# Second aggregation, router, dense mixture and node features in one stage over pairs of node tiles; half the edge products in the edge stage

## The chip, the cores and the metric

One core of one Trainium2 chip. The metric is the device time of one launch in microseconds (us); lower is better. In the profile PE is TensorE, PEld its weight loads, DVE is VectorE, ACT is ScalarE, POOL is GpSimd, and SP issues most transfers.

## The reference, cut to what matters

6250 nodes (49 tiles of 128, `NT`) with 256 features; 106250 edges sorted by destination. Four layers, each added to `x`:

```python
h = relu(segment_sum((LN(x) @ W1)[src] * w, dst) + b1)          # conv 1, hidden 128
x = x + segment_sum((h @ W2)[src] * w, dst) + b2                # conv 2
f = LN(x)                                                        # mixture of 6 experts, top 2
top_w, top_i = top_k(softmax(relu(f @ rw1 + rb1) @ rw2 + rb2), 2)
x = x + sum_k softmax(top_w)[k] * (relu(relu(f @ e1 + c1) @ e2 + c2) @ e3 + c3)[top_i[k]]
n = mish(LN(x) @ Wd.T + bd)                                      # node features
msg = relu(n[src] + mish(edge_attr @ We.T + be))                 # 106250 edges x 256
x = x + mish((n + segment_sum(msg, dst)) @ Wo.T + bo)
x = x + moe8(LN(x))                                              # 8 experts, top 2, H = 512
```

`mish(z)` is `z * tanh(softplus(z))`.

## The kernel before

Everything is in float32, so that one multiplication of the source is two records in the trace. Edges are padded to 840 columns of 128 and handled in groups of four columns (`CG`), 208 groups (`GROUPS`) in all. The gathering stages loop over steps of six groups (`SLOTS`), 34 full steps and one of four (`TAIL`). POOL gathers the source rows of a group with four indirect transfers into one of six buffers, and goes on when DVE has released a buffer (`slot_free`). A group's destinations lie in one window of 64 nodes (`W`): DVE builds one-hot matrices (`one_hots`), TensorE multiplies them with the gathered rows (`segment`), and DVE adds the result to a table in SBUF at the group's place (`add`). The places are loaded from SBUF into registers six at a time (`places_of`). The whole loop runs `passes` times, once unless a group's span is wider than 64.

`build` calls the stages one after another, with a barrier between them:

- `stage_begin`: loads `x` (all 49 tiles stay in SBUF), normalises it, multiplies with `W1` and stores the support table; DVE finds each group's first destination.
- `stage_conv(0)`: first aggregation. Beside it runs half of the edge products, independent work: for 105 of the 210 groups the edge attributes are loaded, multiplied with `We` (`product`), and turned into minus mish by `mish_begin` (DVE: bias, bound), `mish_factor` (four ACT passes of 1024 elements) and `mish_end` (DVE), and stored to DRAM.
- `stage_hidden`: bias, relu, transpose, store of the hidden table; POOL adds `b2` to `x` in seven pieces.
- `stage_conv(1)`: second aggregation, with the other half of the edge products beside it.
- `stage_dispatch(0)`: tile units of four: `W2`, layer norm, router, ranks of the chosen rows, scatter of rows to the experts' regions.
- `stage_experts(0)`: per expert, halves of 256 rows: transpose, three layers, scatter-add into `mixed_nodes`; two of six experts per node are computed.
- `stage_nodes`: loads `x` again, layer norm, `Wd`, mish, stores the node table and keeps minus its transpose in SBUF.
- `stage_edges`: per group gather, add of the stored minus mish (loaded by SP), ACT's rectification `rectified`, `segment` (eight multiplications of 64 columns), `add`.
- `stage_dispatch(1)`, `stage_experts(1)`: the last mixture.

Within a stage each engine runs its own instructions in order; the order is written out by hand, in `step` functions, with semaphores between the engines (`take` waits and counts down).

The order in which DVE worked in the edge stage was, for each of the six groups:

```python
for s in range(slots):
    message(k, i, s)          # one-hots, wait for the gather, node row - mish
    add(places[s], (s - 1) % SLOTS)
```

Of the kernel before, what the change touches and what calls it, by code (L numbers as in the profile page):

```python
# [5 lines left out]
FP32 = mybir.dt.float32  # L6
# [7 lines left out]
P = 128  # L14
D = 256
# [33 lines left out]
ZMAX = 20.0  # L49
SHARES = D  # L50
# [7 lines left out]
LAST = N - WHOLE * P  # L58

# [44 lines left out]
class Chip:  # L104


    def __init__(self, nc, ctx, io):
        self.nc, self.io = nc, io
        sb = lambda name, shape, dt=FP32: ctx.enter_context(nc.sbuf_tensor(name, shape, dt))
        self.x = sb("x_sb", [P, T, D])  # L110
# [14 lines left out]
        self.gb2 = sb("gb2_sb", [P, D])  # L125
# [4 lines left out]
        self.mish_d = dram("edge_mish_table", (EG, P, CG, D))  # L130
# [5 lines left out]
    def feature_table(self, name):  # L136

        return FeatureTable(self, name)


class FeatureTable:


    def __init__(self, c, name):
        self.c, self.name = c, name

    def __enter__(self):
        self.held = self.c.nc.sbuf_tensor(self.name, [P, KD, TW], FP32)
        self.c.feat = self.held.__enter__()
# [5 lines left out]
def stage_begin(nc, c):  # L155
# [4 lines left out]
    with ExitStack() as ctx:  # L160
# [5 lines left out]
        dst_gf = sb("dst_gf", [EGP, 2, CG * P])  # L166
        low, high, span = sb("low", [EGP, 2]), sb("high", [EGP, 2]), sb("span", [EGP, 2])
# [13 lines left out]
        pt_ready, xt_ready, py_ready, rows_ready = sem("pt_ready"), sem("xt_ready"), sem("py_ready"), sem("rows_ready")  # L181
        rows_out = [sem(f"rows_out{r}") for r in range(2)]
# [3 lines left out]
        def _(sp):  # L186
# [8 lines left out]

            load(0)
            sp.dma_start(c.ident[:], io["ident"]).then_inc(ident_in, 16)
            load(1)
            sp.dma_start(w1[:], io["g_w1"]).then_inc(w_in, 16)
            for u in range(2, U):  # L200
                load(u)
            sp.dma_start(c.src[:], io["src_t"]).then_inc(later_in, 16)
# [3 lines left out]
            sp.dma_start(c.gb2[:], io["g_b2"]).then_inc(later_in, 16)  # L206
            for u in range(U):
                store(u)
            sp.wait_ge(later_in, 5 * 16)
# [4 lines left out]
        def _(pool):  # L214
# [10 lines left out]
            pool.dma_start(span_1[:], c.span_d.rearrange("(a g) -> a g", a=1)).then_inc(spans_in, 16)  # L225

        @block.vector
        def _(dve):
# [27 lines left out]
            def relative():  # L256
# [8 lines left out]
                nc.vector.tensor_scalar_add(c.passes[:], shifted[:], 1.0)  # L265
# [91 lines left out]
def stage_conv(nc, c, part, table):  # L357
# [3 lines left out]
    io, name = c.io, f"conv{part}"  # L361
    with ExitStack() as ctx:
# [16 lines left out]
        sums = c.feat[:, 0, :]  # L379
# [13 lines left out]
        def load_passes(eng):  # L393
            return eng.value_load(c.passes[0:1, 0:1], min_val=1, max_val=TW // W)

        @block.sync
        def _(sp):
            group = lambda i, r: bass.ds(i * MISH + (part * IT * MISH + r), 1)

            def load(i, r):  # L400

                take(sp, edge_free[r])
                sp.dma_start(edge[r][:], io["edge_t"][group(i, r)].rearrange("a p k e -> p (a k) e")).then_inc(edge_in[r], 16)

            def store(i, r):
                take(sp, neg_ready[r])
                sp.dma_start(c.mish_d[group(i, r)].rearrange("a p j d -> p (a j) d"), neg[r][:]).then_inc(neg_out[r], 16)
# [33 lines left out]
        def _(dve):  # L441
# [75 lines left out]
            link(dve, nc.vector.memset(sums, 0.0), own)  # L517
# [62 lines left out]
def stage_hidden(nc, c):  # L580

    U, RING = len(UNITS), 4
    with ExitStack() as ctx:
# [7 lines left out]
        block = ctx.enter_context(nc.Block())  # L591
# [11 lines left out]
        def _(act):  # L603
            for u, (t, n) in enumerate(UNITS):
                if u >= RING:
                    act.wait_ge(ps_ready, u - RING + 1)
                act.activation(hid[u % RING][:, 0:n * P], c.feat[:, 0, t * P:(t + n) * P], ACT.Relu, bias=c.gb1[:]).then_inc(hid_ready, 1)
# [19 lines left out]
        @block.gpsimd  # L627
        def _(pool):
            for t in range(0, NT, 7):
                nodes = c.x[:, t:t + 7, :]  # L630
                nc.gpsimd.tensor_tensor(nodes, nodes, c.gb2[:].unsqueeze(1).to_broadcast([P, 7, D]), ALU.add)


def stage_experts(nc, c, mix, target):


# [291 lines left out]
def stage_nodes(nc, c):  # L928

    io = c.io
    U = len(UNITS)
    with ExitStack() as ctx:
# [799 lines left out]
```

## Time and profile before

| | us |
|---|---|
| median of 3 runs | 4712.82 (4711.4 to 4717.11) |
| span of the profiled execution | 4705.9 |
| first convolution, from its first gather to the hidden stage | 88.9 to 1150 |
| hidden | 1150 to 1180 |
| second convolution | 1180 to 2240 |
| first dispatch / its experts / node features | 184 / 381 / 156 |
| edge stage | 2961 to 4041 |
| last dispatch / its experts | 204 / 461 |

Busy shares over the span: PE 72%, PEld 63%, DVE 50%, ACT 37%, POOL 63%; mean granted clock of TensorE 0.751 of 2.4 GHz. The profile has no time of its own for what lies outside the span; the difference to the median, 7 us, is taken for it.

A share over the span is a mean over stages with different limits, so the stage table is read before it. Matmuls are pipelined, and a busy PE is not PE at its peak; the clock column says at which of its two levels (1.2 and 2.4 GHz) it ran, as a mean.

### The profile page before, as it was taken

What the parts mean: (1) busy time and instruction counts of PE and PEld (TensorE: products, weight loads), DVE (VectorE), ACT (ScalarE), POOL (GpSimd) and SP (SyncE); (2) the same over time, 40 slices, a digit from 0 to 9 for tenths busy, and PEclk for the clock granted to TensorE, in tenths of its full rate; (3) what the DMA queues carried; (4) which work ended last, traced back from release to release, by engine and by line L of the source; (5) the groups of instructions that cost most, each with busy time, mean ns of one, the idle gap of its engine ahead of it and who ended that gap; (6) DMA issues with size and microseconds to landing.
All of it is one profiled execution on the core that took longest, in us unless ns stands there. A gap on an engine that the chain in (4) does not pass through costs nothing. (4 is left out here: it accounts for less than half of the span.)

```text
span 4705.9 us, 62078 instructions
## 1 busy us (share of the span) xinstructions
PE 3378.5 (72%) x15159; PEld 2951.3 (63%) x15159; DVE 2342.6 (50%) x6879; ACT 1726.5 (37%) x2410; POOL 2947.3 (63%) x2924
## 2 busy tenths in 40 slices
PE   5777767775677776776658866577767776667999
PEld 5666656664566665665446655566666666556887
DVE  5565555554566555555653335344443444582222
ACT  4444444443444444444323237222222222452333
POOL 2777777777677777777454430677777777363434
PEclk8777888787778888888769988555555555668999
DMA  4455554554455455544345541566666666234443
GB/s 139 153 162 160 157 162 156 158 155 131 150 162 162 153 160 159 160 151 144 110 123 89 107 100 58 177 205 204 204 206 204 205 205 201 92 129 119 97 91 63
DMA packets 317645, 696.83 MB, mean 148 GB/s; under 512 B 67233, under 2 KB 172091, under 8 KB 317420
## 3 DMA queue, kind: packets, MB, share of 16 engines
q1 hardware_dynamic: 170748, 402.05, 25.4%
q0 software_dynamic: 134560, 272.09, 23.9%
q10 hardware_dynamic: 12240, 21.66, 1.4%
q14 instruction: 69, 0.57, 0.0%
q8 instruction: 28, 0.46, 0.0%
HBM read 499.16 MB, written 198.82 MB: 148 GB/s over the span
## 5 line engine op out<-in xcount | busy, mean ns | idle before, releaser
L1151 POOL DMA_INDIRECT x_node<-node_table,src_sb x832 | 814.2, 979 | 411.8 <-issue 405.4
L562 PE MATMUL conv_pz<-conv_we,conv_edge 128*128 128x256 f32 x3360 | 1007.4, 467 | 44.6 <-PEq L76 44.6
L1165 PE MATMUL x_pa<-x_hot,x_node 128*128 128x64 f32 x3328 | 751.7, 423 | 328.4 <-PEq L76 327.7
L434 POOL DMA_INDIRECT conv_gath<-support_table,src_sb x832 | 787.8, 947 | 315.5 <-issue 302.9
L553 PE MATMUL conv_ps<-conv_hot,conv_gath 128*128 128x64 f32 x3328 | 550.3, 326 | 584.1 <-PEq L76 302.3
L434 POOL DMA_INDIRECT conv_gath<-hidden_table,src_sb x832 | 787.4, 946 | 263.8 <-issue 251.4
L1165 PEld LDWEIGHTS x_pa<-x_hot,x_node 128*128 128x128 f32 x3328 | 723.5, 331 | 356.8 <-issue 356.7
L553 PEld LDWEIGHTS conv_ps<-conv_hot,conv_gath 128*128 128x128 f32 x3328 | 516.0, 237 | 652.8 <-issue 340.8
L562 PEld LDWEIGHTS conv_pz<-conv_we,conv_edge 128*128 128x128 f32 x3360 | 796.2, 243 | 188.5 <-issue 45.9
L876 ACT ACTIVATE conv_q<-conv_q 128x1024 f32<-128x1024 f32 x210 | 221.9, 1057 | 1104.8 <-ACTq L76 1104.8
L1180 ACT ACTIVATE x_node<-x_node 128x1024 f32<-128x1024 f32 x208 | 219.7, 1056 | 856.1 <-ACTq L76 856.1
L1199 DVE TENSOR_TENSOR x_node<-x_node,x_neg 128x256 f32<-128x256 f32 x832 | 298.6, 420 | 309.5 <-DMA x_node<-node_table,src_sb 308.6
L445 DVE TENSOR_TENSOR conv_pz<-conv_pz,conv_bias 128x1024 f32<-128x1024 f32 x210 | 258.8, 1232 | 282.1 <-DVEq L76 282.1
L470 DVE SCALAR_TENSOR_TENSOR conv_hot<-iota_sb,conv_at_hot 128x64 f32<-128x64 f32 x1680 | 343.5, 278 | 21.3 <-DVEq L76 11.0
L682 POOL DMA_INDIRECT out<-e_outs,e_node x112 | 173.5, 1550 | 284.2 <-POOLq L76 267.2
L723 PE MATMUL e_ph<-e_xt,e_w_first 128*128 128x256 f32 x1304 | 306.1, 385 | 58.5 <-PEq L76 53.8
L462 DVE TENSOR_TENSOR sums_table<-sums_table,conv_ps 128x64 f32 x416 | 92.2, 222 | 506.0 <-DVEq L76 506.0
L1321 POOL DMA_INDIRECT expert_rows<-r_xn,r_row x196 | 194.6, 993 | 209.0 <-issue 94.8
L723 PEld LDWEIGHTS e_ph<-e_xt,e_w_first 128*128 128x128 f32 x1304 | 246.6, 192 | 108.5 <-issue 76.7
L682 POOL DMA_INDIRECT mixed_nodes<-e_outs,e_node x102 | 157.5, 1544 | 228.8 <-POOLq L76 213.3
L446 DVE TENSOR_SCALAR conv_q<-conv_pz 128x1024 f32<-128x1024 f32 x210 | 257.1, 1224 | 31.4 <-DVEq L76 0.3
L453 DVE SCALAR_TENSOR_TENSOR conv_neg<-conv_q,conv_pz 128x1024 f32<-128x1024 f32 x210 | 253.9, 1209 | 34.0 <-DVEq L76 34.0
(197 smaller groups left out, 3873.8 us busy)
## 6 DMA issues: line engine op xcount, KB each, us to landing
conv_edge<-in_edge_t SPq DMA_DIRECT2D x210, 512.0 KB
edge_mish_table<-conv_neg SPq DMA_DIRECT2D x210, 512.0 KB, 3.0
x_neg<-edge_mish_table SPq DMA_DIRECT2D x208, 512.0 KB, 3.9
e_rows<-expert_rows SPq DMA_DIRECT2D x107, 272.0 KB, 3.3
conv_gath<-support_table,src_sb POOLq DMA_INDIRECT x832
conv_gath<-hidden_table,src_sb POOLq DMA_INDIRECT x832
x_node<-node_table,src_sb POOLq DMA_INDIRECT x832
expert_rows<-e_zeros ACTq DMA_DIRECT2D x12, 544.0 KB, 3.8
```

The source lines that it names most:

```text
L434: pool.indirect_dma_start(gath[g % SLOTS][:, j, :], None, table[:, :], bass.IndirectOffsetOnAxis(ap=c.src[:, col:col + 1], axis=0),).then_ ...
L445: link(dve, nc.vector.tensor_tensor(ps_z[r][:], ps_z[r][:], bias[:].unsqueeze(1).to_broadcast([P, CG, D]), ALU.add), neg_own)
L446: nc.vector.tensor_scalar(q[r][:], ps_z[r][:], ZMAX, None, ALU.min).then_inc(z_ready[r], 1)
L453: link(dve, nc.vector.scalar_tensor_tensor(neg[r][:], q[r][:], -1.0, ps_z[r][:], ALU.add, ALU.mult), neg_own)
L470: last = nc.vector.scalar_tensor_tensor(hot[half][:, j, :], c.iota[:], at_hot[half][:, 0, j:j + 1], at_hot[half][:, 1, j:j + 1].to_broadca ...
L553: last = pe.matmul(ps[s % 2][:], gath[s][:, j, :], hot[half][:, at + j, :], start=j == 0, stop=j == CG - 1)
L562: last = pe.matmul(ps_z[r][:, j, :], edge[r][:, m, j * P:(j + 1) * P], we[:, m, :], start=m == 0, stop=m == KD - 1)
L682: pool.indirect_dma_start(target[:, :], bass.IndirectOffsetOnAxis(ap=node[:, s:s + 1], axis=0), outs[:, s, :], None, compute_op=ALU.add, * ...
L723: last = pe.matmul(ps_h[m][:], w_first[e][:, k, m * P:(m + 1) * P], xt[:, k, :], start=k == 0, stop=k == KD - 1)
L1151: pool.indirect_dma_start(node[g % SLOTS][:, j, :], None, c.t3[:, :], bass.IndirectOffsetOnAxis(ap=c.src[:, col:col + 1], axis=0),).then_i ...
L1165: last = pe.matmul(ps_a[n][:, m, :], node[s][:, j, m * P:(m + 1) * P], hot[n][:, j, :], start=j == 0, stop=j == CG - 1)
L1199: last = nc.vector.tensor_tensor(node[s][:, j, :], node[s][:, j, :], neg[s % RING][:, j, :], ALU.add)
```

## The change

`stage_conv(1)`, `stage_dispatch(0)`, `stage_experts(0)` and `stage_nodes` become one stage, `stage_mixing`. It gathers and sums the hidden rows as before, but without edge products, and follows the nodes in 27 parts (`PARTS`: two single tiles, 22 pairs, three single tiles). Part `u` may be used once the first `DUE[u]` groups are summed. For each part all six experts are computed densely and weighted with shares that are zero except for the chosen two. One iteration of six steps (one per expert) interleaves four parts: groups summed for part `u+2`; support, norm, router of `u+1`; experts of `u`; node features of `u-1` and `u-2`. It is unrolled. Edge products: the first convolution still does 105, the edge stage now does 104 itself (odd groups), and reads the other half from DRAM. POOL's addition of `b2` moves to the first stage, whose `x` is stored as `biased_nodes` and read again part by part. `passes` gets one more when a part's tiles would be used too early (`rows_needed`).

```diff
+PARTS = (1, 1) + (2,) * 22 + (1, 1, 1)
+DUE = tuple(min(GROUPS, -(-E * (t + n) // (N * CG)) + SLACK) for t, n in PARTS)
@@ stage_begin
+            def keep(u):
+                sp.wait_ge(biased, u + 1)
+                sp.dma_start(c.biased_d[...], c.x[:, t:t + n, :]).then_inc(biased_out, 16)
...
             for u in range(U):
                 store(u)
+                if u:
+                    keep(u - 1)
+            for u, (t, n) in enumerate(UNITS):
+                pool.wait_ge(xn_ready, u + 1)
+                nc.gpsimd.tensor_tensor(nodes, nodes, gb2[:].unsqueeze(1).to_broadcast([P, n, D]), ALU.add).then_inc(biased, 1)
...
-                nc.vector.tensor_scalar_add(c.passes[:], shifted[:], 1.0)
+                chain(nc.vector.tensor_tensor(need[:], need[:], base_1[:], ALU.subtract))
+                chain(nc.vector.tensor_reduce(late[:], need[:], AX.X, ALU.max))
+                nc.vector.tensor_single_scalar(late[:], late[:], 0.0, ALU.is_gt)
+                nc.vector.scalar_tensor_tensor(c.passes[:], shift_f[:], 1.0, late[:], ALU.add, ALU.add)
@@ stage_hidden
-        @block.gpsimd
-        def _(pool):
-            for t in range(0, NT, 7):
-                nc.gpsimd.tensor_tensor(nodes, nodes, c.gb2[:].unsqueeze(1).to_broadcast([P, 7, D]), ALU.add)
@@ stage_mixing, TensorE
+            def first_layer(u, e):
+                for m in range(KD):
+                    for k in range(KD):
+                        last = pe.matmul(ph[:, m, 0:width(u)], w_1[e][:, k, m * P:(m + 1) * P], xt[u % 2][:, k, 0:width(u)], ...)
+            def step(k, u, j):
+                for g in summed_in(u, j):
+                    segment(k, g)
+                following, earlier = next_of(u, j), earlier_of(u, j)
+                if there(u):
+                    take(pe, hid_ready)
+                if there(following[0]):
+                    first_layer(*following)
+                if j == 0 and there(u + 1):
+                    support(u + 1)
+                if j == 1 and there(u - 2):
+                    turned_back(u - 2)
+                if j == 2 and there(u):
+                    turned_shares(u)
+                if j == 2 and there(u + 1):
+                    turned(u + 1)
+                if j == 3 and there(u + 1):
+                    router(u + 1)
+                if j == 3 and there(u):
+                    shared_bias(u)
+                if j == 3 and there(u - 1):
+                    turned_mixed(u - 1)
+                if j == 4 and there(u + 1):
+                    logits(u + 1)
+                if j == 4 and there(u - 1):
+                    dense(u - 1)
+                if there(earlier[0]):
+                    take(pe, mid_ready)
+                if there(u):
+                    second_layer(u, j)
+                if there(earlier[0]):
+                    third_layer(*earlier)
@@ stage_mixing, DVE
+            def step(u, j):
+                for g in summed_in(u, j):
+                    add(g)              # and one_hots after every third, places_of before every sixth
+                if j == 0: finished(u - 2); supported(u + 1)
+                if j == 1: shared(u); refined()
+                if j == 3: bias_added(u)
+                if j == 4: biased(u + 1); bounded(u - 1)
+                if j == 5: chose(u + 1)
+                weighted(*earlier)
+                if j == 0: mixed(u - 1); moments(u)
@@ stage_edges, TensorE, ACT, DVE
+            def step(products):
+                for r in range(MISH):
+                    segment(2 * r)
+                    segment(2 * r + 1)
+                    if r < products:
+                        product(r)
...
+                    rectified(0)
+                    rectified(1)
+                    factor(2)
+                    rectified(2)
+                    rectified(3)
+                    factor(0)
+                    rectified(4)
+                    rectified(5)
+                    factor(1)
...
+            def step(k, i, places, before):
+                message(k, i, 0)
+                if before:
+                    add(places[0], SLOTS - 1)
+                at = places[before:]
+                mish_end(0)
+                message(k, i, 1)
+                add(at[0], 0)
+                mish_begin(2)
+                message(k, i, 2)
+                add(at[1], 1)
+                mish_end(1)
+                message(k, i, 3)
+                add(at[2], 2)
+                mish_begin(0)
+                message(k, i, 4)
+                add(at[3], 3)
+                mish_end(2)
+                message(k, i, 5)
+                add(at[4], 4)
+                mish_begin(1)
...
+            for t in range(0, NT, LATER):
+                sp.dma_start(c.x[:, t:t + LATER, :], c.mixed_d[...]).then_inc(x_in, 16)
@@ build
-            stage_conv(nc, c, 1, c.t2)
-            stage_dispatch(nc, c, 0, c.mixed_d)
-        stage_experts(nc, c, 0, c.mixed_d)
...
-            stage_nodes(nc, c)
-            stage_edges(nc, c)
+                stage_mixing(nc, c, c.t2)
+            with c.table("nodes", [P, T, D]):
+                stage_edges(nc, c)
```

(DVE's `step` of the mixing stage is abridged: the conditions that a part exists are left out.)

TensorE in the mixing stage, two steps (experts 4 and 5) of an iteration over pairs, of the changed kernel. `x_ps` are segments, `x_ph`, `x_pm`, `x_py` the three expert layers, `x_pu` the router, `x_px` the node product:

```order
L1105 MATMUL x_ps<-x_hot,x_gath 128x64 x4
L1171 MATMUL x_ph<-x_xt,x_w 128x256 x4
L1133 MATMUL x_pu<-x_w_l,x_rh 128x6 x2
L1160 MATMUL x_px<-x_w_d,x_xt 128x256 x4
L1177 MATMUL x_pm<-x_hid,x_w 128x256 x4
L1184 MATMUL x_py<-x_w,x_mid 128x256 x4
L1105 MATMUL x_ps<-x_hot,x_gath 128x64 x8
L1171 MATMUL x_ph<-x_xt,x_w 128x256 x4
L1177 MATMUL x_pm<-x_hid,x_w 128x256 x4
L1184 MATMUL x_py<-x_w,x_mid 128x256 x4
```

Before, a stage that gathers had segments and edge products here; now the expert layers of another part stand between the segments of one or two groups.

DVE in the edge stage, start of a step, before:

```order
L354 TENSOR_LOAD x_window
L354 ISA x12
L1193 ISA
L1193 TENSOR_TENSOR x_hot<-iota_sb,x_rel 128x256
L1197 ISA
L1199 TENSOR_TENSOR x_node<-x_node,x_neg 128x256 x4
L1208 ISA
L1208 TENSOR_TENSOR messages_table<-messages_table,x_pa 128x2x64
```

and of the change:

```order
L403 TENSOR_LOAD y_window
L403 ISA x12
L1694 ISA
L1694 TENSOR_TENSOR y_hot<-iota_sb,y_rel 128x256
L1700 ISA
L1702 TENSOR_TENSOR y_node<-y_node,y_neg 128x256 x4
L1712 ISA
L1712 TENSOR_TENSOR messages_table<-messages_table,y_pa 128x2x64
L1689 SCALAR_TENSOR_TENSOR y_q<-y_q,y_pz 128x1024
```

Three of `mish_end` (L1689) and three of `mish_begin` (L1684, L1685) now stand in a step between the additions and the messages.

## Rows read from the trace of the kernel before

**Rows 1.** View by windows, one window for each stage; columns in its first line
```profile
core 0: us, PE busy (x) PEld busy (x) DVE busy (x) ACT busy (x) POOL busy (x), PEclk, DMA share, GB/s
1150.00:1180.00 30.00, 9.20 (x49) 8.19 (x49) 9.13 (x17) 8.46 (x15) 27.59 (x7) 0.61 0.39 108
1180.00:2240.00 1060.00, 750.42 (x3344) 642.76 (x3344) 616.82 (x1508) 454.75 (x421) 787.41 (x832) 0.81 0.50 156
2240.00:2424.00 184.00, 111.68 (x414) 80.78 (x414) 124.18 (x749) 59.33 (x140) 95.39 (x98) 0.69 0.33 115
2424.00:2805.00 381.00, 304.44 (x1428) 252.27 (x1428) 133.49 (x361) 108.38 (x306) 157.48 (x102) 0.97 0.50 93
2805.00:2961.00 156.00, 94.99 (x392) 78.38 (x392) 78.47 (x220) 111.17 (x170) 0.00 (x0) 0.76 0.26 85
2961.00:4041.00 1080.00, 751.66 (x3328) 723.50 (x3328) 438.28 (x1252) 219.71 (x208) 814.21 (x832) 0.50 0.65 202
4245.00:4706.00 461.00, 428.06 (x2016) 365.93 (x2016) 121.25 (x340) 156.53 (x449) 173.89 (x113) 0.97 0.45 91
```

**Rows 2.** Timeline of POOL in the edge stage: two gathers in a row
```profile
3205.09 0.95 POOL L1151 DMA_INDIRECT x_node<-node_table,src_sb  x1 [0.30 <-issue]
3206.34 0.95 POOL L1151 DMA_INDIRECT x_node<-node_table,src_sb  x1 [0.30 <-issue]
```

**Rows 3.** Timeline of TensorE in the last stage, at full clock
```profile
4400.27 3.62 PE L723 MATMUL e_ph<-e_xt,e_w_first 128*128 128x256 f32 x16
4403.73 0.60 PE L347 MATMUL e_pt<-ident_sb,e_rows 128*128 128x128 f32 x4
4407.84 3.62 PE L723 MATMUL e_ph<-e_xt,e_w_first 128*128 128x256 f32 x16
```

**Rows 4.** Timeline of TensorE in the second convolution stage
```profile
1701.81 1.11 PE L553 MATMUL conv_ps<-conv_hot,conv_gath 128*128 128x64 f32 x8 [2.12 <-DMA conv_gath<-hidden_table,src_sb]
1702.75 5.36 PE L562 MATMUL conv_pz<-conv_we,conv_edge 128*128 128x256 f32 x16
1720.36 3.45 PE L553 MATMUL conv_ps<-conv_hot,conv_gath 128*128 128x64 f32 x16 [4.37 <-PEq L76]
```

**Rows 5.** Timeline of DVE and ACT in the second convolution: one edge product's mish
```profile
1708.35 1.23 DVE L445 TENSOR_TENSOR conv_pz<-conv_pz,conv_bias 128x1024 f32<-128x1024 f32 x1 [1.19 <-DVEq L76]
1709.73 1.23 DVE L446 TENSOR_SCALAR conv_q<-conv_pz 128x1024 f32<-128x1024 f32 x1
1711.08 1.06 ACT L876 ACTIVATE conv_q<-conv_q 128x1024 f32<-128x1024 f32 x1 [4.58 <-ACTq L76]
1714.62 1.15 ACT L879 ACTIVATE conv_q<-conv_q,conv_ln 128x1024 f32<-128x1024 f32 x1
```

**Rows 6.** Timeline of the edge stage: one group, and the load of places
```profile
3182.36 0.29 DVE L1208 TENSOR_TENSOR messages_table<-messages_table,x_pa 128x128 f32 x1
3186.52 0.42 DVE L1193 TENSOR_TENSOR x_hot<-iota_sb,x_rel 128x256 f32<-128x256 f32 x1 [3.88 <-issue]
3186.86 1.43 DVE L1199 TENSOR_TENSOR x_node<-x_node,x_neg 128x256 f32<-128x256 f32 x4
...
3203.50 1.06 ACT L1180 ACTIVATE x_node<-x_node 128x1024 f32<-128x1024 f32 x1 [5.77 <-ACTq L76]
3204.70 3.65 PE L1165 MATMUL x_pa<-x_hot,x_node 128*128 128x64 f32 x16 [3.18 <-PEq L76]
3208.78 0.29 DVE L1208 TENSOR_TENSOR messages_table<-messages_table,x_pa 128x128 f32 x1 [0.51 <-DVEq L76]
3209.31 0.43 DVE L1193 TENSOR_TENSOR x_hot<-iota_sb,x_rel 128x256 f32<-128x256 f32 x1 [0.24 <-DVEq L76]
```

**Rows 7.** View by groups of instructions: DVE one-hots, POOL's bias addition, a DVE pass of 512
```profile
L470 DVE SCALAR_TENSOR_TENSOR conv_hot<-iota_sb,conv_at_hot 128x64 f32<-128x64 f32 x1680 | 343.5, 278 | 21.3 <-DVEq L76 11.0
L631 POOL TENSOR_TENSOR x_sb<-x_sb,gb_sb 128x1792 f32<-128x1792 f32 x7 | 27.6, 3977 | 12.4 <-POOLq L101 12.4
L850 DVE TENSOR_TENSOR e_plain<-e_py,e_b_last 128x512 f32<-128x512 f32 x107 | 73.1, 683 | 0.0
```

More of the change, by code:

```diff
@@ L49 @@
 ZMAX = 20.0
+PIECE = 2
+SLACK = 2
 SHARES = D
@@ new lines, in _ @@
+        @block.gpsimd
+        def _(pool):
+            with pool.Fori(0, load_passes(pool)) as k:
+                for g in range(GROUPS):
+                    if g >= SLOTS:
+                        pool.wait_ge(slot_free, g - SLOTS + 1)
+                    for j in range(CG):
+                        col = g * CG + j
+                        pool.indirect_dma_start(
+                            gath[g % SLOTS][:, j, :], None, table[:, :],
+                            bass.IndirectOffsetOnAxis(ap=c.src[:, col:col + 1], axis=0),
+                        ).then_inc(gathered[g % SLOTS], 16)
+                take(pool, slot_free, GROUPS)
@@ L1204, in add @@
                 dve.sem_inc(slot_free, 1)
-                dve.sem_inc(neg_free[s % RING], 1)
+                if s % 2 == 0:
+                    dve.sem_inc(neg_free[s // 2], 1)
                 here = c.feat[:, :, bass.ds(at, W)]
-                link(dve, nc.vector.tensor_tensor(here, here, ps_a[s % RING][:], ALU.add), add_own)
-            def step(k, i, slots):
-                places = places_of(nc, window, i * SLOTS - 1, slots, whole=True)
-                for s in range(slots):
-                    message(k, i, s)
-                    add(places[s], (s - 1) % SLOTS)
+                link(dve, nc.vector.tensor_tensor(here, here, ps_a[s % 2][:], ALU.add), own)
@@ new lines, in last_step @@
+            def last_step(k, i):
+                places = places_of(nc, window, i * SLOTS - 1, TAIL + 1, whole=True)
+                message(k, i, 0)
+                add(places[0], SLOTS - 1)
+                mish_end(0)
+                message(k, i, 1)
+                add(places[1], 0)
+                message(k, i, 2)
+                add(places[2], 1)
+                mish_end(1)
+                message(k, i, 3)
+                add(places[3], 2)
+                add(places[4], 3)
+            for r in range(MISH):
+                dve.sem_inc(z_free[r], 1)
@@ L1216, in _ @@
+            link(dve, nc.vector.memset(ln2[:], LN2), own)
+            dve.sem_inc(consts_ready, 1)
             nc.vector.tensor_copy(rel[:], c.dstrel[:])
-            link(dve, nc.vector.tensor_copy(window[:], c.base[:]), add_own)
+            link(dve, nc.vector.tensor_copy(window[:], c.base[:]), own)
+            dve.wait_ge(w_in, 32)
             with dve.Fori(0, load_passes(dve)) as k:
-                places = places_of(nc, window, 0, SLOTS)
-                for s in range(SLOTS):
-                    message(k, 0, s)
-                    if s:
-                        add(places[s - 1], s - 1)
+                mish_begin(0)
+                mish_begin(1)
+                step(k, 0, places_of(nc, window, 0, SLOTS - 1), 0)
```

813 lines of the change are left out of this document (594 added, 219 removed).

## The prediction

> **What bounds the kernel now.** I read the view by windows first, one window a stage [rows 1]. Two stages gather 832 times over the hidden table and the node table: the second convolution (1180 to 2240 us) and the edge stage (2961 to 4041). In both POOL is the busiest engine that never rests for others: a gather starts every 1.25 us (3205.09 to 3206.34) [rows 2], so a group of four takes 5.0 us and 208 groups 1040 us, against 1060 and 1080 for the stages. TensorE has slack there, at a mean clock of 0.81 of 2.4 GHz in one and 0.50 (1.2 GHz throughout) in the other. Between them lie the dispatch (184 us), the experts (381) and the node features (156), in which hardly anything gathers. The last stage shows TensorE as the bound: 428 of 461 us busy, clock 0.97 [rows 1].
>
> **What is removed.** From the second convolution's start to the edge stage's start: 1060 + 184 + 381 + 156 = 1781 us [rows 1]. The hidden stage (30 us) was held open by POOL's bias addition, 27.6 us in seven pieces [rows 7]; its other engines show 9 us of work [rows 1]. The addition moves to the first stage, so some 13 us go here.
>
> **First stage.** POOL was idle there after its few transfers, but the addition to a unit waits for that unit's normalisation and is followed by a store on SP behind the support rows. A unit of four tiles costs POOL 27.6 x 4/49 = 2.3 us; what shows is the last unit and its store, +3 us. Bounds: 0 (hidden) and +27.6 (none hidden). The one row of POOL's addition ran beside DVE passes that read PSUM, so nothing here prices it beside DVE passes over SBUF. The Trainium skill (GPSIMD Engine Reference, Key points) says POOL shares its SBUF interfaces with VectorE and contends with instructions of two SBUF inputs; by that the term goes to its upper bound, +27.6. I keep +3: few DVE passes of that stage have two large inputs.
>
> **Mixing stage, TensorE.** Prices at full clock come from the last stage [rows 3]: 16 records of 256 columns from 4400.27 to 4403.73, 0.216 us each (a multiplication is two records), a transpose 0.145 (0.58 for four). A record of 64 columns costs 0.94/8 = 0.118 (1701.81 to 1702.75) [rows 4]. A part of two tiles has, by the order shown, six experts x 12 multiplications of 256 columns, 2 for the support, 2 router, 2 shared bias, 4 dense = 82, or 164 records: 35.4 us. Fourteen transposes add 2.0, the two small logits 0.5. So 37.9 us without segments; 8.5 groups a part bring 68 records, 8.0 us. **Sum 45.9 us a part, against 8.5 x 5.0 = 42.5 us for its gathers**: TensorE becomes the bound, narrowly.
>
> In time order: parts 0 and 1 are single tiles, and their steps wait for gathers up to group 29: 29 x 5.0 + 3 = 148 us. Then 22 full parts: 22 x 37.9 = 834, with 179 groups x 8 x 0.118 = 169: 1003 us. Three single parts follow, 18 steps of about 2.7 us of TensorE and a handoff, some 3.3 us each: 60 us. The last part's node features run alone: normalise, transpose, product, mish: 15 us. Stalls: the steps put every handoff one step apart, so most are covered by 7 us of other multiplications. DVE per part: 34 one-hots at 343.5/1680 = 0.20, nine passes the size of L850 at 0.68 [rows 7], twelve weighted additions about 0.45, 8.5 sums additions about 0.75, small chained operations about 8, and 1.4 loads of places at 3.88 [rows 6]: about 38 us, estimated from these rows, 83% of TensorE's time. A step with a load and a one-hot batch overruns by some 3 us; where it lies on moments, deviation, spreading and transposing, TensorE waits. I take 3 us a part, +66 (bounds 0, TensorE never waiting, and 11 a part, DVE's waits added in series). **Mixing: 148 + 1003 + 66 + 60 + 15 = about 1292 us**, bounds 1220 and 1470. Weights (4.7 MB) land within the first 140 us.
>
> **Edge stage.** It now computes 104 products, one for every second group. Its gathers need 30 us a step of six groups. But the order makes a ring through three engines, three times a step: mish_begin on DVE, the factor on ACT, the rectification behind it on ACT, the segment on TensorE, the addition on DVE, and only then the next mish_begin. Its price: bias and bound until ACT starts 2.73 us (1708.35 to 1711.08), factor 4.69 (1711.08 to 1714.62 + 1.15) [rows 5], 0.1 between, rectification to addition 5.28 at half clock (3203.50 to 3208.78), addition to the next start 0.53 [rows 6]. That is 13.3 us; at full clock the segment's 3.65 us becomes 1.9 and the ring 11.6. I take a segment of 2.5 us, since TensorE rests about 4 us in each turn and was back at the slow pace after 4.37 us of rest (16 records in 3.45 us) but not after 2.12 [rows 4]: 12.2 us. One turn in three also holds the load of places, 3.88 us of DVE [rows 6], in front of the message on which the rectification waits: 0.8 us more, since part of it lies beside the factor: 13.0. So 13.0 + 2 x 12.2 = 37.4 us a step, over the gathers' 30. 34 steps: 1272 us; 20 us ahead (weights, two products and factors before the first message), 17 behind. **1309 against 1081: +228 us.** Bounds: nothing but the gathers and these ends, 0; half clock throughout, 13.3 a turn and TensorE's own 14.2 (two segments and a product of 6.9): +400. The seven reloads of node tiles at the end (6.4 MB at about 200 GB/s, 32 us [rows 1]) start some 36 us before the end and hide.
>
> The Trainium skill (Runtime: NRT & Kernel Launch, Instruction fetch mechanics) puts such a load at about 200 ns a register. The row shows 3.88 us for six registers, 0.65 each, so this trace disagrees. By the page the load would be 1.2 us and leave the ring: the stage would be 34 x 0.8 = 27 us shorter. I use the row.
>
> **Sum.** Profiled span 4705.9 - 1781 - 13 + 3 + 1292 + 228 = 4435; 7 us lie outside the span (the median of the runs shown is 4712.8): **about 4442 us**.
>
> **Rivals.**
> (a) *Edge stage stays at gather pace.* If six slots of lookahead hid the ring: the ring is no latency but a cycle, so lookahead doesn't help it; for it speaks only that conv, with the same factor, keeps pace (there no rectification follows the factor). 4442 - 228 + 20 = 4234. Chance 0.12.
> (b) *Mixing at gather pace.* If TensorE's prices are 8% lower, 208 x 5.0 + 75: 1115, total 4265. Against it: the last stage's period of 7.57 us [rows 3] is measured, not assumed. 0.05.
> (c) *Mixing paced by handoffs.* If DVE and TensorE wait for each other in turn at 8 us a part more: 4442 + 176 = 4618. For it: the experts of before were busy only 304 of 381 us at clock 0.97 [rows 1], with the same layers. 0.15.
> (d) *Slower: TensorE at 1.2 GHz in the mixing stage.* At half clock a part costs 164 x 0.43 + 14 x 0.29 + 68 x 0.22 + 1 = 91 us, 22 x 45 = +990: 5430. It decides once a part costs 45.9 + 3 + 270/22 = 61 us, that is from a third of the work at half clock. For it: the edge stage stayed at 0.50 with TensorE busy 752 of 1080 us. Against: both expert stages show 0.97, and this one leaves less rest. 0.05.
> (e) *It doesn't do what it says.* The new test adds a second pass when a node tile would be used before its edges are in, which doubles three stages: +3600 us. The destinations of the reference's inputs reach over at most 33 nodes in a group and never fall below the tiles already used, so one pass remains. 0.01.
> My forecast keeps 0.62, with its own range 4330 to 4560.
>
> **Numbers.** A measurement of this kernel tells 0.2%, about 9 us, from no change. The range 4250 to 4640 takes in (b) and (c), the upper halves of the unknown terms together (mixing stalls +110, edge ring +90), and leaves out (a), (d), (e) and tails, about 0.2. Faster: the forecast, (a), (b), (c) = 0.94; within 0.2%: 0.01; slower, (d), (e) and far tails of (c): 0.05.
>
> **What would show it.** Right: the mixing stage about 1290 us long, TensorE at clock near 1.0 and busy over 90% from its 150th us, POOL waiting for free slots; the edge stage about 1300 us, DVE additions at intervals of some 12 us per pair, POOL idle a fifth of the time on slots, and its clock well over 0.50. Wrong: gathers in the edge stage at 1.25 us without pauses (a); TensorE idle in every mixing step with DVE the releaser (c); a clock near 0.5 in the mixing stage (d); 1664 gathers a stage (e). The first error I would look for is the ring's segment time and the 3 us of stalls.

## The result, and the profile after

| | us |
|---|---|
| before, median | 4714.04 (4711.4 to 4717.11) |
| after, median | 4379.49 (4372.94 to 4385.57, 4 runs) |
| ratio | 0.929, 95% interval 0.9279 to 0.9301 |
| profiled span after | 4371.1, mean clock of TensorE 0.843 |

The kernel became 335 us faster, where the prediction had 272 (4714 to 4442). The comparison is again read stage by stage. View by windows of the kernel after; the stages are: first, convolution, hidden, the mixing stage in three pieces (single parts ahead, 22 full parts, single parts behind), edges, last mixture:

```profile
core 0: us, PE busy (x) PEld busy (x) DVE busy (x) ACT busy (x) POOL busy (x), PEclk, DMA share, GB/s
0.00:104.00 104.00, 50.64 (x294) 45.82 (x294) 66.48 (x211) 44.41 (x96) 34.39 (x27) 0.80 0.61 178
104.00:1165.00 1061.00, 763.83 (x3344) 653.82 (x3344) 615.73 (x1506) 454.89 (x422) 787.74 (x832) 0.78 0.50 156
1165.00:1182.00 17.00, 8.54 (x49) 6.95 (x49) 8.92 (x17) 7.89 (x15) 0.00 (x0) 0.70 0.68 189
1182.00:1330.00 148.00, 94.36 (x509) 86.48 (x510) 63.16 (x283) 24.24 (x73) 111.97 (x118) 0.67 0.32 96
1330.00:2335.00 1005.00, 978.28 (x5349) 876.15 (x5348) 492.25 (x2097) 380.10 (x895) 682.19 (x715) 0.99 0.24 65
2335.00:2434.00 99.00, 79.08 (x519) 70.19 (x518) 37.25 (x142) 45.86 (x136) 0.00 (x0) 0.92 0.06 19
2434.00:3712.00 1278.00, 1018.78 (x4992) 914.62 (x4992) 796.92 (x1566) 652.35 (x625) 798.23 (x832) 0.77 0.53 176
3712.00:4371.00 659.00, 552.60 (x2566) 470.38 (x2566) 280.31 (x1058) 265.61 (x634) 272.91 (x210) 0.89 0.40 96
```

Three things are to be seen beside [rows 1]. In the 22 full parts TensorE is busy 978 of 1005 us at clock 0.99: it is the bound there, and no gather pace. In the edge stage nobody is: TensorE 1019, POOL 798 and DVE 797 of 1278 us, so something between the engines sets the time. And DVE is busy 66.5 us in the first stage, 48.0 before, where nothing was added for it but some small operations.

The edge stage is read in its timeline (DVE, ACT and TensorE of the kernel after; three turns of the ring the prediction described; the transfers and some other rows are left out):

```profile
3007.40 1.23 DVE L1684 TENSOR_TENSOR y_pz<-y_pz,y_bias 128x1024 f32<-128x1024 f32 x1 [0.35 <-DVEq L91]
...
3016.58 3.68 PE L1621 MATMUL y_pa<-y_hot,y_node 128*128 128x64 f32 x32
...
3019.53 1.23 DVE L1684 TENSOR_TENSOR y_pz<-y_pz,y_bias 128x1024 f32<-128x1024 f32 x1 [0.35 <-DVEq L91]
3020.91 1.23 DVE L1685 TENSOR_SCALAR y_q<-y_pz 128x1024 f32<-128x1024 f32 x1
...
3022.26 1.06 ACT L918 ACTIVATE y_q<-y_q 128x1024 f32<-128x1024 f32 x1 [5.57 <-ACTq L91]
...
3025.78 1.15 ACT L921 ACTIVATE y_q<-y_q,y_ln 128x1024 f32<-128x1024 f32 x1
...
3026.84 1.99 ACT L1655 ACTIVATE y_node<-y_node 128x1024 f32<-128x1024 f32 x2
3028.02 7.06 PE L1621 MATMUL y_pa<-y_hot,y_node 128*128 128x64 f32 x32 [4.25 <-PEq L91]
3032.09 0.29 DVE L1712 TENSOR_TENSOR messages_table<-messages_table,y_pa 128x128 f32 x1 [4.50 <-DVEq L91]
3032.72 1.23 DVE L1684 TENSOR_TENSOR y_pz<-y_pz,y_bias 128x1024 f32<-128x1024 f32 x1 [0.35 <-DVEq L91]
...
3044.23 1.23 DVE L1684 TENSOR_TENSOR y_pz<-y_pz,y_bias 128x1024 f32<-128x1024 f32 x1 [0.35 <-DVEq L91]
```

From one bias (L1684) to the next there is a closed chain, with ACT idle 5.57 us, TensorE 4.25 and DVE 4.50 in turn, each waiting for the one before it. The turns are 12.13 and 13.19 us; the second pays segments at about half the pace (7.06 us for 32 records, against 3.68 for the 32 from 3016.58). The third turn of a step is 11.51 us, which makes 36.8 us here. Over the whole stage the 104 biases start from 2446.6 to 3684.2, which is 36.1 us a step; the three turns take 12.6, 11.6 (the one with the load of places) and 11.8 us in the mean.

In the first stage one group of DVE stands out. View by groups of instructions, stage one, after (before, the same operation of 128x4 took 0.144 us):

```profile
L269 POOL TENSOR_TENSOR nodes_table<-nodes_table,b_gb 128x1024 f32<-128x1024 f32 x10 | 23.7, 2378 | 21.1 <-ACT b_xn L958 21.1
L948 DVE TENSOR_TENSOR b_work<-b_guess 128x4 f32<-128x4 f32 x10 | 15.3, 1532 | 1.0 <-ACT b_guess L942 1.0
L305 DVE CAST base_row<-b_base 1x210 int32<-1x210 f32 x1 | 2.4, 2362 | 0.0
```

An operation on four elements a partition takes 1.5 us. The timeline of the same stage says why:

```profile
37.26 7.37 DVE L948 TENSOR_TENSOR b_work<-b_guess 128x4 f32<-128x4 f32 x1
37.69 6.92 POOL L269 TENSOR_TENSOR nodes_table<-nodes_table,b_gb 128x1024 f32<-128x1024 f32 x3
```

DVE's operation ends at 44.63, POOL's third addition in a row at 44.61. The first two of these additions ended at 40.02 and 42.31 without letting it through. Six more of the 15 such operations of the stage took 0.40 to 2.00 us, and each ended 0.02 or 0.03 us after an addition of POOL's.

### The profile page after: what moved, and what is told of

It is laid out like the page before. It is cut to its first block and busy times, and to the rows that moved or that the text cites. A ratio compares the mean times of both kernels' runs of the same rounds, so it can differ in the third digit from the quotient of the medians.

```text
span 4371.1 us, 66370 instructions
## 1 busy us (share of the span) xinstructions
PE 3546.1 (81%) x17618; PEld 3124.4 (71%) x17618; DVE 2361.0 (54%) x6877; ACT 1875.4 (43%) x2892; POOL 2687.4 (61%) x2732
## 5 line engine op out<-in xcount | busy, mean ns | idle before, releaser
L1608 POOL DMA_INDIRECT y_node<-node_table,src_sb x832 | 798.2, 959 | 573.5 <-issue 348.6
L1088 POOL DMA_INDIRECT x_gath<-hidden_table,src_sb x832 | 794.2, 955 | 361.8 <-issue 268.2
L1621 PE MATMUL y_pa<-y_hot,y_node 128*128 128x64 f32 x3328 | 544.8, 339 | 250.5 <-PEq L91 250.5
L1621 PEld LDWEIGHTS y_pa<-y_hot,y_node 128*128 128x128 f32 x3328 | 530.4, 252 | 284.2 <-issue 282.8
L609 PE MATMUL conv_pz<-conv_we,conv_edge 128*128 128x256 f32 x1680 | 511.3, 472 | 18.1 <-PEq L91 18.1
L1631 PE MATMUL y_pz<-y_we,y_edge 128*128 128x256 f32 x1664 | 497.6, 465 | 8.5 <-PEq L91 8.5
L609 PEld LDWEIGHTS conv_pz<-conv_we,conv_edge 128*128 128x128 f32 x1680 | 402.9, 246 | 92.9 <-issue 18.8
L1631 PEld LDWEIGHTS y_pz<-y_we,y_edge 128*128 128x128 f32 x1664 | 395.0, 244 | 79.1 <-issue 8.9
L1171 PE MATMUL x_ph<-x_xt,x_w 128*128 128x256 f32 (+1 forms) x1296 | 296.3, 373 | 0.7 <-PEq L91 0.6
L1177 PE MATMUL x_pm<-x_hid,x_w 128*128 128x256 f32 (+1 forms) x1296 | 290.8, 369 | 2.0 <-PEq L91 1.9
```

Source lines behind the costliest of these rows:

```text
L609: last = pe.matmul(ps_z[r][:, j, :], edge[r][:, m, j * P:(j + 1) * P], we[:, m, :], start=m == 0, stop=m == KD - 1)
L1088: pool.indirect_dma_start(gath[g % SLOTS][:, j, :], None, table[:, :], bass.IndirectOffsetOnAxis(ap=c.src[:, col:col + 1], axis=0),).then_ ...
L1171: last = pe.matmul(ph[:, m, 0:width(u)], w_1[e][:, k, m * P:(m + 1) * P], xt[u % 2][:, k, 0:width(u)], start=k == 0, stop=k == KD - 1)
L1177: last = pe.matmul(pm[:, m, 0:width(u)], w_2[e][:, k, m * P:(m + 1) * P], hid[e % 2][:, k, 0:width(u)], start=k == 0, stop=k == KD - 1)
L1608: pool.indirect_dma_start(node[g % SLOTS][:, j, :], None, c.t3[:, :], bass.IndirectOffsetOnAxis(ap=c.src[:, col:col + 1], axis=0),).then_i ...
L1621: last = pe.matmul(ps_a[s % 2][:, m, :], node[s][:, j, m * P:(m + 1) * P], hot[s % MISH][:, j, :], start=j == 0, stop=j == CG - 1)
```

## The experiments

Twelve kernels were run; the one before ran beside each set on the same chip at 4708 to 4710 us. Comparisons below are against 4379 us and the stages of after. The kernel after was not run again beside them, and the one before had 4714 in its set, so a difference of totals is uncertain by some 5 us; seven kernels ran once only (marked below), and they are judged by their stages. A stage's length is taken from its first gather to the next stage's, and the edge stage's from its first to its last gather (after: 2434.3 to 3680.1, 1246 us; 208 groups at 5.0 us would be 1040).

**Cut the ring.** In `step` of the edge stage DVE does `mish_begin` ahead of the addition that it followed. Nothing is left out.

```diff
                 message(k, i, 1)
+                mish_begin(2)
                 add(at[0], 0)
-                mish_begin(2)
...
                 message(k, i, 3)
+                mish_begin(0)
                 add(at[2], 2)
-                mish_begin(0)
...
                 message(k, i, 5)
+                mish_begin(1)
                 add(at[4], 4)
-                mish_begin(1)
```

> Edit: in the edge stage VectorE starts each mish (bias and bound) before the addition it followed, so that no factor waits for a segment any more. Theory 1 (the ring DVE, ACT, ACT, TensorE, DVE sets the stage's 36.5 us a step): the ring is cut, the step falls to what is next, the gathers at 30 us a step (ACT needs 26, DVE 23.4). The edge stage goes from 1279 to 1080 to 1130 us, the whole to 4180 to 4235 us. Theory 2 (TensorE itself is the bound: busy 1019 of 1278 us, 14.2 us a pair at half clock): the stage changes by less than 60 us, TensorE busy over 90% of it. Theory 3 (the order of VectorE's work as a whole, 23.4 us busy and the rest handoffs): under 60 us as well, with the idle time of VectorE moved to other waits and TensorE no busier.

Measured: 4203.01 us (4194.97 to 4217.45), ratio to before 0.8928 (0.8906 to 0.895), 176 us less than after; by the two ratios to before it is 171. Windows of this kernel, edge stage:

```profile
2434.60:3542.00 1107.40, 937.80 (x4992) 843.93 (x4992) 795.10 (x1579) 661.95 (x625) 806.92 (x832) 0.81 0.63 204
```

From the first gather to the last 1246 became 1076 us (2434.6 to 3510.5), with the same instructions; three pairs of calls are in another order. That is theory 1; theories 2 and 3 had under 60 us. TensorE was busy 1019 us and is now busy 938 with as many records: it was idle 259 us of the stage at a granted clock of 0.77, and is idle 170 at 0.81.

**No edge products.**

> Leaves out: the edge products, their bias, bound and factor for every second group in the edge stage; the odd messages read the stored minus-mish of the group before them instead, so traffic is the same. Theory 1 (products and the ring they close cost all that the stage grew by): the edge stage falls to the 1080 us of before, the whole to 4180 us (4165 to 4200), gathers every 1.25 us, clock near 0.5. Rival (part of the growth has another cause, such as only two accumulators where there were three, or the bigger hidden cost of loads): the stage stays above 1120 us, the whole above 4220.

Measured: 4184.0 us (one run); gathers of the edge stage from 2439.6 to 3502.0, 1062 us. Windows:

```profile
2439.00:3532.00 1093.00, 758.74 (x3344) 728.00 (x3344) 444.01 (x1276) 224.48 (x215) 810.17 (x832) 0.50 0.66 206
```

Theory 1: total and clock are as it said. Beside the first experiment it says more: 104 products with their mish cost 1076 - 1062 = 14 us once the ring is cut, and 1246 - 1062 = 184 us in it. The 14 is rough, since this stage's gathers differ by 22 us between kernels with the cut ring (below); against 184 the reading holds: the products were not dear, only badly placed. The clock is 0.50, as before, with TensorE idle 334 of 1093 us.

**Less and more TensorE work in the mixing stage.**

```diff
 third_layer (less)
-                    for k in range(KD):
-                        last = pe.matmul(py[:, s, :], mid[e % 2][:, k, ...], w_3[e][:, k, :], start=k == 0, stop=k == KD - 1)
+                    last = pe.matmul(py[:, s, :], mid[e % 2][:, 0, ...], w_3[e][:, 0, :], start=True, stop=True)
 third_layer (more)
+                for again in range(2 if e < 2 else 1):
```

> Leaves out: the second half of the third layer of all six experts in the mixing stage (12 multiplications of 256 columns a full part, 24 records of 0.216 us, 5.2 us of a part's 45.7). Theory 1 (TensorE is the bound, the gathers 42.5 us a part just behind it): the part falls to the gathers' pace only, 22 x 3.2 = 70 us, with the single parts some 75 us: 4305 us (4295 to 4325), POOL without pauses. Rival A (gathers are never next): the full 22 x 5.2 = 114 us, 4260. Rival B (handoffs set the part, TensorE is busy only because its weights loads wait inside): under 30 us, above 4350.

> The third layer of the first two experts is computed twice (8 multiplications of 256 columns more a full part, 16 records of 0.216 us, 3.46 us). Theory 1 (TensorE is the bound in all 22 full parts): 22 x 3.46 = 76 us, with the five single parts about 84: 4463 us (4450 to 4475). Rival B (there is slack in handoffs, 27 us of idle TensorE in those parts): under 55 us, since it fills waits first. Rival C (TensorE is bound in some parts only, gathers in the others): 30 to 60 us.

Measured: 4307.77 us with less, 4429.08 with more (one run each). The pace of a part is read from the support product (L1113 in the kernel after) of the fifth part and of the 24th, 19 parts apart. Timeline of TensorE: kernel after, less, more:

```profile
1376.84 1.03 PE L1113 MATMUL x_px<-x_w_x,sums_table 128*128 128x256 f32 x4
...
2264.97 1.03 PE L1113 MATMUL x_px<-x_w_x,sums_table 128*128 128x256 f32 x4
```

```profile
1377.38 1.03 PE L1113 MATMUL x_px<-x_w_x,sums_table 128*128 128x256 f32 x4
...
2205.79 1.03 PE L1113 MATMUL x_px<-x_w_x,sums_table 128*128 128x256 f32 x4
```

```profile
1382.64 1.03 PE L1113 MATMUL x_px<-x_w_x,sums_table 128*128 128x256 f32 x4
...
2310.94 1.03 PE L1113 MATMUL x_px<-x_w_x,sums_table 128*128 128x256 f32 x4
```

That is 888.1/19 = 46.7 us a part, 43.6 with less and 48.9 with more. Windows over the whole mixing stage, in the same order:

```profile
1182.00:2434.00 1252.00, 1151.72 (x6373) 1032.82 (x6373) 592.66 (x2521) 450.20 (x1103) 794.16 (x832) 0.95 0.23 65
```

```profile
1184.00:2363.00 1179.00, 1042.79 (x5785) 932.49 (x5785) 594.78 (x2522) 448.81 (x1103) 793.58 (x832) 0.93 0.25 69
```

```profile
1184.00:2486.00 1302.00, 1224.19 (x6765) 1102.37 (x6765) 593.24 (x2518) 451.81 (x1103) 793.59 (x832) 0.96 0.22 62
```

With less, the part falls to the gathers and no further: they came at 5.10 us a group (1184.5 to 2246.0 for 208), 43.4 a part, and POOL, which waited 93.6 us for buffers in the full parts of the kernel after, waits 20.8 there. Rival A had 114 us, measured are 72. So TensorE is the bound and the gathers are next, 3.1 us behind: theory 1.

With more, the stage grew by 50 us and not 84. That lies in the range of rival B (under 55) and in that of rival C (30 to 60) as well, so the total doesn't choose between them. The single parts do. From the fifth to the 24th, five parts took 44.5 us in the kernel after, with TensorE never idle; all five took 48.0 with more, so 3.5 us for 16 records, the forecast's price (the sixth part: 1426.28 to 1470.80, then 1432.12 to 1480.10). Four parts took 49.2 us or more, with TensorE idle 2.4 to 3.3 us in each, and grew by 0.1 at most. So TensorE alone sets some parts, as rival C said, and in the others something else does, but not the gathers that C named: TensorE waited 0.4 us for gathered rows in the 22 parts and 24.5 us before transposes (x_pt). The slack is in handoffs, as rival B said. Over the stage TensorE's idle time fell from 100 to 78 us and its busy time grew by 72.5 us: 72.5 - 22 = 50. That is 72.5/392 = 0.185 us for an added record (for a removed one 108.9/588, the same) and not 0.216; where TensorE was never idle it is the full price, so some of what counts as busy in the other parts is waiting too.

**POOL's addition in the first stage.** The next three runs price it, move it in time, and change what it is.

```diff
 moved in time
                 pool.wait_ge(xn_ready, u + 1)
+                pool.wait_ge(rstd_ready, min(u + 2, U))
 left out
-                nc.gpsimd.tensor_tensor(nodes, nodes, gb2[...], ALU.add).then_inc(biased, 1)
+                pool.sem_inc(biased, 1)
 copy
-                nc.gpsimd.tensor_tensor(nodes, nodes, gb2[...], ALU.add).then_inc(biased, 1)
+                nc.gpsimd.tensor_copy(nodes, nodes).then_inc(biased, 1)
```

> Edit: in the first stage POOL's bias addition to a unit waits in addition for the deviation of the next unit, so that it starts after VectorE's five small operations on SBUF and beside its moments and its copy. Theory 1 (VectorE's first small two-input operation waits until POOL's addition ends: 15.3 us over ten units where it took 1.4 us before, one of 7.37 us that ended with three additions in a row): those operations return to 0.15 us and the first gather starts at 90 to 94 us in place of 103.8, total -10 to -14 us: 4365 to 4370. Rival (the stores of the biased nodes on SP's queue hold up the support rows): no change, within 4 us of 4379.

> Leaves out: the bias addition to the node features in the first stage (the store of them stays, at the same point). Theory 1: the first gather starts at 89 to 92 us as before (88.9), total -12 to -15 us, VectorE's small operations at 0.15 us. Rival (stores, or the longer queue of SP): stays near 103 us.

> Leaves out: the bias addition of the first stage; POOL copies each unit onto itself in its place (one SBUF input in place of two). Tells what on POOL blocks VectorE. Theory A (any POOL operation over SBUF holds up VectorE's small two-input operations): they still end with POOL's copies, first gather above 100 us where those last as long. Theory B (only a POOL operation with two SBUF inputs does): they return to 0.15 us, first gather at 91 to 94 us as without the addition, total 4366 to 4372.

| | total | first gather at |
|---|---|---|
| before | 4714 | 88.9 |
| after | 4379 | 103.8 |
| moved in time | 4373.02 (4370.81 to 4374.66) | 100.5 |
| left out, one run | 4368.61 | 91.4 |
| copy, one run | 4376.43 | 96.8 |

The totals hardly tell these kernels apart (moved in time: ratio to before 0.9288, and 0.929 for the kernel after), so the first gather decides. In seven kernels with the same first stage it lies between 103.8 and 106.5 us. Leaving the addition out gives back 12.4 of the 15 us; the remaining 2.5 are no more than that spread, and what they are (the stores, their place in SP's queue, the added small operations) is not separated. Moving the addition in time gave back only 3.3: my 10 to 14 missed, since POOL reaches its first addition behind its small transfers, at 36 us, with four units waiting, and does them in one burst. The groups of that kernel show DVE's operation at 6.8 us in all in place of 15.3, 5.48 of it in one wait; without waits they are 1.4. Of the four operations that write `dstrel` one took 2.41 us, which makes 1.00 in the mean in place of 0.53. That is 5.4 + 1.9 of the 9.1 us by which the gather lies above 91.4, if all of it stands in the way of the gather, which no run shows. The copy decides between theories A and B. Timeline of the kernel with the copy:

```profile
37.11 4.11 POOL L269 COPY nodes_table<-nodes_table 128x256 f32<-128x256 f32 x5
39.26 1.98 DVE L948 TENSOR_TENSOR b_work<-b_guess 128x4 f32<-128x4 f32 x1
```

The copies end at 41.22, DVE's operation at 41.24. A POOL operation with one SBUF input holds it up too: theory A. (Its first gather, at 96.8, lies between the two theories' figures, which fits its shorter operations: 1.04 us a unit in place of 2.38.)

**The load of places, twice.** In the middle steps of the edge stage `places_of` is called a second time, in the kernel after and in the one with the cut ring.

> The kernel after, with the load of six places done twice in each of the 33 middle steps of the edge stage (VectorE, ring uncut). My price of a load is 3.88 us from the idle time beside it, with 0.8 us of it in the ring; a second load has no cover of its own. Theory 1 (a load costs 3.9 us in the ring): 33 x 3.9 = +129 us, 4508 us. Theory 2 (it costs the 2.55 us of idle time that the trace of after shows at that place): +84 us, 4463. Theory 3 (some 200 ns a register): +40 us, 4419. If all of the second load lay beside the factor: 0.

> The same double load in the kernel with the cut ring (e1, 4203 us; edge stage 1107 us). If the cut ring leaves VectorE slack against the gathers (30 us a step, of which VectorE is busy 23.4), the load hides: under +30 us. If VectorE was the next bound, it costs as much as in the uncut one, +84 to +129 us.

Measured (one run each): 4514.68 us, +135, in the ring: 4.1 us a step, theory 1. With the cut ring 4300.96, +98: 3.0 a step, the number of the case in which DVE is next in line; my "under 30 us" fell. So the cut ring has little slack left on DVE; with one load its turns take 9.0, 12.2 and 9.8 us in the mean, and the longest is the one with the load. DVE's row at that place in the kernel after, then in the doubled one:

```profile
3037.88 0.43 DVE L1694 TENSOR_TENSOR y_hot<-iota_sb,y_rel 128x256 f32<-128x256 f32 x1 [2.55 <-issue]
```

```profile
3023.15 0.43 DVE L1694 TENSOR_TENSOR y_hot<-iota_sb,y_rel 128x256 f32<-128x256 f32 x1 [5.65 <-issue]
```

One load shows 2.55 us of idle time, two show 5.65. The turn with the load takes 11.6 us in the mean of the kernel after, less than the other two, and 15.7 with two (in the doubled kernel the biases around one start at 2974.16 and 2990.18). So in the uncut ring one load hides beside ACT's factor and the second doesn't.

**Together, and two attempts to go on.**

> The cut ring of the edge stage and the shifted addition of the first stage together. If both theories hold the gains add, since the stages follow each other: 4379 - (150 to 200) - (10 to 14) = 4165 to 4219 us. If either falls, this shows the other alone.

> As e7, and two things more. First stage: POOL adds the bias to the first four units before and between its small transfers, since the shifted addition showed them bunched behind these (7.07 us of additions in a row from 35.99 us, VectorE's small operation waiting 5.48 of them). Mixing stage: SLACK 1 in place of 2, so that each part begins one group of gathers (5.0 us) earlier; with these destinations one pass is still enough. Theory 1: first gather at 92 to 95 us in place of e7's 99.2, mixing 1245 us in place of 1250, total 4175 to 4188. Rival (the first stage is held by SP's queue, whose stores wait behind loads until some 35 us, and not by VectorE's waits): first gather above 97 us, and total within 5 us of e7.

> Cut ring and SLACK 1 as in e8, and no addition on POOL at all: the first stage stores no biased nodes, the mixing stage loads the node features as they came in, and VectorE adds the bias there (one operation of 512 columns a part, about 0.7 us, ahead of its wait for the support product), where it is busy 492 of 1005 us. Theory 1 (the first stage pays for POOL's additions and their store): first gather at 89 to 91 us against e8's 96.6, mixing within 4 us of e8's 1237, since the addition fills VectorE's waits: 4163 to 4170 us. Rival (the addition delays the support's handoff by 0.7 us a part, and TensorE waits): mixing up to 15 us longer, total 4170 to 4185.

| | total | ratio to before | first gather | mixing | edge stage's gathers |
|---|---|---|---|---|---|
| cut ring + addition moved | 4194.28 (4183.32 to 4210.56) | 0.8914 (0.89 to 0.8929) | 99.2 | 1250.3 | 1069 |
| + first additions early, `SLACK` 1 | 4172.81 (4168.8 to 4197.39) | 0.8875 (0.8854 to 0.8897) | 96.6 | 1237.0 | 1066 |
| cut ring, `SLACK` 1, bias added by DVE in mixing | 4195.52 (4190.76 to 4202.93) | 0.8911 (0.8899 to 0.8923) | 87.3 | 1250.4 | 1088 |

(Last column: from the stage's first to its last gather.) In the first line the two gains add up, within what was expected (4165 to 4219). The second line is the fastest found, 207 us under the kernel after, 196 by the ratios. Its total lies 2 us under its range, its first stage missed again (96.6, not 92 to 95), and its mixing stage gained 13 us where one group earlier explains 5: the full parts took 46.3 us each in place of 46.6, and why is open. The third line is the instructive one. Its first stage fell by 9 us, a little further than theory 1 said (87.3, not 89 to 91). But the mixing stage gave 13 us back, as its rival said: an operation of 0.69 us a part on DVE, the engine busy half the time, sits on the way from the support product to the normalisation. From the end of that product to DVE's addition of it 1.60 us pass in the second line's kernel and 2.31 in this one (means of the 27 parts). And the edge stage, whose code is the same in all three lines, took 20 us more, so that the total came out above the rival's 4170 to 4185 too. The gathers of that stage lie between 1066 and 1088 us in four kernels with the cut ring; what decides it is open, and so the 21 us between the first two lines are not all to be put down to the edits.

## Why the prediction was right, and where its terms were off

The prediction's path and mechanisms held: TensorE bounds the mixing stage narrowly, and the ring bounds the edge stage. Its terms were off as follows, mostly in the same direction, so little of the hit is errors that cancel.

**Removed, 1781 us:** gone, and nothing came in its place. Hidden stage: 13 forecast, 12 measured (29.7 to 17.6 us). First convolution (1061) and last mixture (664 before, 659 after): unchanged, as assumed.

**First stage, +3: wrong, +15.** The step that failed is "few DVE passes of that stage have two large inputs". It is not their size: passes of four elements pay, and each carries the unit's chain, which goes deviation, spreading, transposing. The measured 15 us lie in the upper half of the bounds. That the addition holds up DVE was what the Trainium skill's page said and I weighed too lightly; the 27.6 us that I took from that rule were nearly twice too much. The Trainium skill's page SBUF — State Buffer (section "SBUF: two separate sides") goes further than the page I weighed: the shared port pair is an exclusive lock held for the whole instruction, and the other side fully blocks. The two pairs of end times above agree, and go beyond it: DVE's operation, begun at 37.26, was let through at the end of the third addition and not at that of the one in progress.

**Mixing, 1292 against 1252.** Forecast were 1003 + 66 = 1069 us for the 22 full parts; the trace has 46.7 a part, 1027 us. That leaves 225 us for the single parts and the tail, forecast 148 + 60 + 15 = 223. TensorE's own work was right: it is busy 97.3% of the full parts, 45.5 us of a part. The mis-sized term is the stalls: 66 us forecast, 1005 - 978 = 27 measured. Waits in the full parts (us in total, times, longest):

```profile
PE x_pt L966 <- PEq L91: 24.5, 15, 2.8
POOL x_gath L1088 <- DVEq L1364: 93.6, 47, 10.1
```

The stalls sit where the prediction put them, before the transposes of the normalised rows, but only 15 times in the 22 parts and for at most 2.8 us. One of the terms behind the 3 us a part was too big: DVE was put at 38 us a part, 5.4 of them loads, and is busy 492 us in 1005, or 22.9 a part. That this is why the waits are short is likely and not shown. That TensorE is the bound "narrowly" is shown by the run with less. Rivals (b) and (c) fell with it; the clock of 0.99 refutes (d), 832 gathers refute (e).

**Edge stage, 1309 against 1278.** The ring is shown, by cutting it. Its pace was forecast 37.4 us a step and is 36.1, which makes 44 us over 34 steps; the ends of the stage took some 14 us more than the 37 forecast. The 0.8 us for the load of places were not there: the turn with the load is the shortest of the three, and only a second load shows. The segment was taken at 2.5 us; the trace has 1.8 (3.68 for 32 records), 2.73 and 3.5 (7.06 for 32). Rival (a), gather pace, was wrong for this order of rows and nearly right for another: 4234 was its time, 4203 came out with the ring cut.

On the load itself I used the row against the Trainium skill (Runtime: NRT & Kernel Launch, Instruction fetch mechanics, some 200 ns a register). The row was nearer: the second load adds 5.65 - 2.55 = 3.1 us of idle time, 0.52 a register, and 4.1 us a step. (The page has its figure from registers loaded from HBM; these words lie in SBUF.)

Sum of the errors: +12 (first stage), -40 (mixing), -31 (edges), -5 (last mixture, taken as unchanged): -64, and the profiled span of 4371.1 against the forecast 4435 is -64. The 7 us outside the span were a misreading: a run's time is 1.7 to 2.5 us longer than its own span in every run here, and the rest of the 7 is that the profiled execution was faster than the median. The kernel after shows the same (4379.5 - 4371.1 = 8.4), so this cancelled.

## What to carry to other kernels

When an engine's program alternates between finishing one item and starting the next, look whether the start waits for the finish of something it doesn't need: lookahead in buffers doesn't help a cycle, an exchange of two rows does (some 170 us here). Where nobody is busy and nobody is at gather pace, draw the cycle and add it up before costing anything else. And an engine "busy half the time" is no free place for work: 0.7 us a part on the way between two handoffs cost 13 us, more than the 9 us it saved elsewhere.

## What was not expected of the hardware

A DVE operation on 128x4 elements waited until POOL's work on SBUF ended (7.37 us for a pass of 0.14), for additions and for copies alike. Where POOL had its next operation ready, the wait went on through that one as well: through three additions in a row here. A cast of 210 elements, with a single input, took 2.36 us in place of 0.25 and ended 0.13 us after an addition. `bn_stats` in the same stage did not wait: 0.412 us before and after, beside additions too.

A second one is about cost by company. The edge stage with the ring cut and 104 products ran at a granted clock of 0.81, and the one without products at 0.50: 4992 records in 938 us of busy time against 3344 in 759. So half as many records again took 24% more busy time, in a stage 14 us longer by its gathers.
